# Two attention layers on one core: the output projections in halves, and an accumulating transfer in layer 1

## The chip, the cores and the metric

The kernel runs on one NeuronCore of a Trainium2 chip. The metric is the device time of one execution in microseconds (us), the median of several runs. The engines are TensorE (PE; its weight loads are PEld), VectorE (DVE), ScalarE (ACT), GpSimd (POOL) and SyncE (SP), each with its own instruction stream in program order; they meet by semaphores.

## The reference, cut to what matters

Two blocks follow each other on a sequence of 2048 tokens of width 128, with 16 heads of 64. Each is `x = x + attention(layernorm(x)) * silu(ffn(layernorm(x)))`. The attention of layer 0 is plain; that of layer 1 has rotated queries and keys and a distance bias per head. What this case is about is the last step of attention:

```python
attn = softmax(scores)                              # layer 1: softmax(scores + bias)
out  = einsum('bhqk,bhkd->bhqd', attn, v)
out  = out.transpose(0, 2, 1, 3).reshape(b, s, h * d) @ w_out   # sum over heads of o_h @ W_h
```

The product with the output weights is taken head by head, divided by the row sum of the softmax, and added up over the heads.

## The kernel before, in words

`attention_stage` runs once for each layer. A layer is a loop over 64 chunks (`NCH`), each one head and 512 queries (`NC` is 4 chunks per head, `LAST` is 63), and a chunk is 8 steps (`NS`) of 256 keys. Names: `st` are the scores in PSUM (two buffers), `jb` the PSUM scratch for the maxima, `ov` the attention output in PSUM, `osb` its copy in SBUF, `xb` one PSUM tile of 512 columns, `prob` a ring of six buffers of exponentials (printed as `room`), `acc` the accumulator of all tokens, `part` one chunk's scaled projection, `rs` the inverted row sums.

Each engine's order is written out by hand:

- TensorE, for every two steps: `maxima` two chunks ahead (L649, L650, into `jb`), `scores` (L683), `maxima`, then what `between` adds, then `values` of two steps earlier (L694). `between` has the three users of `xb`: `row(n+1)` in step 3 (L658) turns the chunk's maxima into a row, `sums_of(n-1)` in step 5 (L705) sums the exponentials over partitions, and `project(n-1)` in step 7 (L714) makes the four products of 128 by 128 with the output weights.
- VectorE: per step one maximum (L839 in layer 0, L834 with the bias in layer 1) and, in layer 1, the bias add from `st` into `prob` (L871); in layer 0 every second step a subtraction (L858). `merge` (L845) joins a chunk's maxima. `invert` (L877) makes `rs` from `xb`. In layer 0 `accumulate` (L886) reads `xb` in step 7 and adds it, scaled, to `acc`.
- ScalarE: `exponent` per step (L773, L777, L784), `divide_maxima` (L761) and `copy_out` (L791) in step 0, `row` (L766) in step 2, and in layer 1 `scale` (L798) in step 7, which writes `part` from `xb`.
- GpSimd: per chunk seven adds of 1024 columns over the exponentials (L991 six times, L994), one of 512 (L999), and in layer 1 `add_part` (L978), which adds `part` to `acc`.
- SyncE loads the next head's queries, keys and bias.

`xb` is shared, so its users wait for each other: `row` waits until the projection two chunks back has been read (`proj_done`), `sums_of` until the last one has been read, `copy_out` until the projection has read `osb` (`proj_ready`). `scale` waits until `part` has been added (`accumulated`). In the last chunk there are no maxima to make ahead, VectorE does part of GpSimd's adds (`close`, L912) and then the end: `gate_block` (L897) and `add_block` (L903).

Of the kernel before, what the change touches and what calls it, by code (L numbers as in the profile page):

```python
# [18 lines left out]
NC = S // QC  # L19
# [523 lines left out]
def attention_stage(nc, k, layer, heads, gate, bias=False, out=None):  # L543

    with ExitStack() as ctx:
# [38 lines left out]
        loads = low_loads + (1 if bias else 0)  # L584
        FIRST = AHEAD * NJ
        pool_adds = NS - 1
        block = ctx.enter_context(nc.Block())

        def scratch(n, j):
# [47 lines left out]
        def _(pe):  # L637
# [15 lines left out]
            def row(n):  # L653
                pe.wait_ge(m4_done, n + 1)
                if n >= 3:
                    pe.wait_ge(proj_done, n - 2)
                for t in range(4):
                    last = nc.tensor.matmul(xb[:, t * P:(t + 1) * P], m4w[:, t, :], k.ident16[:, :],  # L658
                                            start=True, stop=True)
                last.then_inc(row_ready, 1)  # L660
# [38 lines left out]
            def sums_of(n):  # L699
                pe.wait_ge(folded, n + 1)  # L700
                pe.wait_ge(row_done, min(n + 3, NCH))
                if n >= 1:
                    pe.wait_ge(proj_done, n)
                for q in range(4):
                    last = nc.tensor.matmul(xb[:, q:q + 1], total[:, q * P:(q + 1) * P], k.ones[:, 0:1],  # L705
                                            start=(q == 0), stop=True, skip_group_check=True)
                last.then_inc(sum_ready, 1)

            def project(n):
                pe.wait_ge(ov_saved, n + 1)  # L710
                pe.wait_ge(rs_done, n + 1)
                pe.wait_ge(row_done, min(n + 3, NCH))
                for q in range(4):
                    last = nc.tensor.matmul(xb[:, q * P:(q + 1) * P], osb[:, q * P:(q + 1) * P], k.wo[:, n // NC, :],  # L714
                                            start=True, stop=True)
                last.then_inc(proj_ready, 1)
# [12 lines left out]
            def between(n, s):  # L729
                if s == ROW_STEP and n + 1 < NCH:  # L730
                    row(n + 1)
                if s == SUM_STEP and n >= 1:
                    sums_of(n - 1)
                if s == OUT_STEP and n >= 1:
                    project(n - 1)

            for n in range(NCH):
                for s in range(NS):
# [9 lines left out]
                        values(*divmod(step - LAG + 1, NS))  # L748
            for s in range(NS - LAG, NS):
                values(NCH - 1, s)  # L750
            sums_of(NCH - 1)
            project(NCH - 1)

        @block.scalar
        def _(act):
            def divide_maxima(n):
                act.wait_ge(merged, n + 1)
                if n >= 1:
                    act.wait_ge(row_ready, n)
                wide = m4w[:, :, 0:DH + 1:DH] if bias else m4w[:, :, :]  # L760
                nc.scalar.activation(wide, m4[:, :].unsqueeze(2).broadcast_to([P, 4, 2 if bias else P]), ACT.Copy,  # L761
                                     scale=1.0 / MAXROW).then_inc(m4_done, 1)

            def row(n):
                act.wait_ge(row_ready, n + 1)
                nc.scalar.activation(rows[:, n % 2, :], xb[:, :], ACT.Copy).then_inc(row_done, 1)  # L766

            def exponent(n, s):
                step = NS * n + s
                r = step % RING  # L770
                if bias:
                    act.wait_ge(added, step + 1)
                    nc.scalar.activation(prob[:, r, :], prob[:, r, :], ACT.Exp, scale=k.sscale[:, layer:layer + 1])\  # L773
                       .then_inc(exp_done, 1)
                elif not by_row(step):
                    act.wait_ge(lowered, step // 2 + 1)
                    nc.scalar.activation(prob[:, r, :], prob[:, r, :], ACT.Exp, scale=k.sscale[:, 0:1])\  # L777
                       .then_inc(exp_done, 1)
                else:
                    act.wait_ge(st_ready, step + 1)  # L780
                    if step >= RING:
                        act.wait_ge(pv_done, step - RING + 1)
                        act.wait_ge(summed, summed_by(step - RING))
                    nc.scalar.activation(prob[:, r, :], st[:, step % 2, :], ACT.Exp, scale=k.sscale[:, layer:layer + 1])\  # L784
                       .then_inc(exp_done, 1)

            def copy_out(n):
                act.wait_ge(pv_done, NS * (n + 1))
                if n >= 1:
                    act.wait_ge(proj_ready, n)  # L790
                nc.scalar.activation(osb[:, :], ov[:, :], ACT.Copy).then_inc(ov_saved, 1)  # L791

            def scale(n):
                act.wait_ge(proj_ready, n + 1)
                if n >= 1:
                    act.wait_ge(accumulated, n)
                for q in range(4):
                    last = nc.scalar.activation(part[:, q * P:(q + 1) * P], xb[:, q * P:(q + 1) * P], ACT.Copy,  # L798
                                                scale=rs[:, q:q + 1])
                last.then_inc(proj_done, 1)  # L800

            act.wait_ge(ones_set, 2)
            nc.scalar.activation(osb[:, 0:1], k.ones[:, 0:1], ACT.Exp)
            divide_maxima(0)
            row(0)
            if bias:
                act.wait_ge(gathered, 16 * NT)
                for q in range(NT):
                    nc.scalar.activation(k.gate[:, q, :], k.gate[:, q, :], ACT.Silu, scale=k.prob[:, q:q + 1])
            for n in range(NCH):  # L810
                for s in range(NS):
                    if s == 0 and n + 1 < NCH:
                        divide_maxima(n + 1)
                    exponent(n, s)
                    if s == 0 and n >= 1:
                        copy_out(n - 1)
                    if s == ROW_STEP - 1 and n + 1 < NCH:
                        row(n + 1)
                    if bias and s == OUT_STEP and n >= 1:
                        scale(n - 1)  # L820
            copy_out(NCH - 1)

        @block.vector
        def _(ve):
# [48 lines left out]
            def invert(n):  # L873
                ve.wait_ge(sum_ready, n + 1)
                if n >= 1:
                    ve.wait_ge(proj_done, n)
                nc.vector.reciprocal(rs[:, :], xb[:, 0:4]).then_inc(rs_done, 1)  # L877

            def accumulate(n):
                ve.wait_ge(ones_set, 3)  # L880
                ve.wait_ge(proj_ready, n + 1)
                if bias:
                    ve.wait_ge(accumulated, n - NC + 1)
                for q in range(4):
                    a = k.acc[:, (n % NC) * 4 + q, :]
                    last = nc.vector.scalar_tensor_tensor(a, xb[:, q * P:(q + 1) * P], rs[:, q:q + 1], a,  # L886
                                                          ALU.mult, ALU.add)
                last.then_inc(proj_done, 1)

            def gate_block(i):  # L890
                block_end = LAST - NC + blocks[i].stop // 4
                if bias and block_end < LAST:
                    ve.wait_ge(accumulated, block_end + 1)
                else:
                    ve.wait_ge(proj_done, block_end + 1)
                tiles = blocks[i]
                nc.vector.tensor_tensor(k.acc[:, tiles, :], k.acc[:, tiles, :], gate[:, tiles, :], ALU.mult)\  # L897
                  .then_inc(finished, 1)
# [29 lines left out]
            for n in range(NCH):  # L928
                if n + 1 < NCH:
                    merge(n + 1)  # L930
                for s in range(NS):
# [6 lines left out]
                    if s == SUM_STEP and n >= 1:  # L938
                        invert(n - 1)
                    if not bias and s == OUT_STEP and n >= 1:  # L940
                        accumulate(n - 1)
                    if n == LAST and s in (6, 7):
                        close(s - 1)
            close(7)
# [4 lines left out]
            if bias:  # L949
                gate_block(1)  # L950
                add_block(1)
            accumulate(LAST)
            gate_block(len(blocks) - 1)
            add_block(len(blocks) - 1)

# [1 line left out]
        def _(pool):  # L957
# [13 lines left out]
            def add_part(n):  # L971
                if n == 0:
                    pool.wait_ge(ones_set, 3)
                pool.wait_ge(proj_done, n + 1)
                if n >= NC:
                    pool.wait_ge(accumulated, n - NC + 1)
                a = flat(k.acc[:, (n % NC) * 4:(n % NC + 1) * 4, :])
                nc.gpsimd.tensor_tensor(a, a, part[:, :], ALU.add).then_inc(accumulated, 1)  # L978

            for n in range(NCH):  # L980
                adds = (1, 3) if n == LAST else (1, 3, 4, 5, 6, 7)
                for i, s in enumerate(adds):
# [6 lines left out]
                        pool.wait_ge(folded, n)  # L989
                    first = a if i >= 2 else prob[:, (step - 1) % RING, :]  # L990
                    nc.gpsimd.tensor_tensor(a, first, prob[:, step % RING, :], ALU.add).then_inc(summed, 1)  # L991
                pool.wait_ge(summed, pool_adds * n + len(adds))
                a = sums[:, n % 2, :]
                nc.gpsimd.tensor_tensor(a, a, sums[:, (n + 1) % 2, :], ALU.add).then_inc(summed, 1)  # L994
                if n < LAST:
# [1 line left out]
                    if n >= 1:  # L997
                        pool.wait_ge(sum_ready, n)
                    nc.gpsimd.tensor_tensor(total[:, :], a[:, 0:QC], a[:, QC:2 * QC], ALU.add).then_inc(folded, 1)  # L999
                if bias and n >= 1:  # L1000
                    add_part(n - 1)


# [563 lines left out]
```

## Time and profile before

| | us |
|---|---|
| median of 3 runs (2865.01 to 2867.71) | 2866.11 |
| the profiled execution | 2865.61 |
| its span, first to last instruction | 2863.8 |
| PE busy / DVE / ACT / POOL | 2715.1 / 2453.7 / 1578.9 / 2459.9 |
| mean granted TensorE clock | 0.974 of full |

Layer 0's chunks lie between about 195 and 1360 us of the span, the feed-forward and rotation stages of layer 1 up to about 1580, and layer 1's chunks from about 1610 to 2850. Busy times are sums over stages with different limits, so the stages have to be looked at one by one. An idle time in square brackets is that of the engine just before the instruction, with what ended it; TensorE's matmuls overlap each other, so that its waits show on PEld or as gaps between starts.

### The profile page before, as it was taken

Reading aid. Unit: us, or ns where it says so; the run is one execution under the profiler, and the core shown is the slowest. Engines: PE = TensorE matmul, PEld = TensorE weight load, DVE = VectorE, ACT = ScalarE, POOL = GpSimd, SP = SyncE. Lnnn points to the kernel's source line nnn. Section 1 sums busy time; section 2 is a strip of 40 time slices with the busy share of each in tenths; the row PEclk is TensorE's granted clock in tenths of the full one; section 3 lists DMA queues with packets and bytes.
Section 4 is the critical chain, followed back from the end, with each engine's and each line's share of the span. In section 5 each row is a group of like instructions: output and inputs, shape, how many; then the busy total and the mean of one; then the engine's idle time right before and its main releaser. Section 6 shows DMA issues by size and latency. Waiting matters only on the chain. (4 is left out here: it accounts for less than half of the span.)

```text
span 2863.8 us, 46490 instructions
## 1 busy us (share of the span) xinstructions
PE 2715.1 (95%) x17528; PEld 1130.0 (39%) x17528; DVE 2453.7 (86%) x3263; ACT 1578.9 (55%) x1970; POOL 2459.9 (86%) x1179
## 2 busy tenths in 40 slices
PE   4899999999999999999589599999999999999998
PEld 3434334433343434433365133333333333333343
DVE  6578888888888888886678699999999999999997
ACT  4345555555555555555255355655565565555555
POOL 0219999999999999999245599999999999999998
PEclk8999999999999999999699699999999999999999
DMA  5441111111111111110323421111222222222200
GB/s 117 145 153 31 30 30 30 31 30 27 26 27 25 27 27 26 29 30 1 97 106 140 142 59 59 56 33 36 53 59 59 59 59 59 59 59 59 59 1 15
DMA packets 68864, 155.27 MB, mean 54 GB/s; under 512 B 20497, under 2 KB 34202, under 8 KB 66466
## 3 DMA queue, kind: packets, MB, share of 16 engines
q1 hardware_dynamic: 67618, 150.21, 18.8%
q8 instruction: 140, 2.29, 0.4%
q0 software_dynamic: 1024, 2.10, 0.2%
q14 instruction: 82, 0.67, 0.1%
HBM read 113.34 MB, written 38.93 MB: 53 GB/s over the span
## 5 line engine op out<-in xcount | busy, mean ns | idle before, releaser
L991 POOL TENSOR_TENSOR a_sums<-a_sums,room 128x1024 f32<-128x1024 f32 x504 | 1179.3, 2368 | 9.0 <-ACT room L773 3.7
L694 PE MATMUL a_ov<-room,va 128*64 128x512 f32 x4096 | 991.6, 605 | 0.6 <-ACT room L773 0.6
L773 ACT ACTIVATE room<-room,sscale 128x1024 f32<-128x1024 f32 x512 | 588.4, 1149 | 493.5 <-DVE room L871 493.3
L839 DVE TENSOR_REDUCE a_mx<-a_jb 128x1 f32<-128x1024 f32 x496 | 606.0, 1222 | 180.3 <-PE a_jb L650 180.1
L991 POOL TENSOR_TENSOR a_sums<-room 128x1024 f32<-128x1024 f32 x256 | 604.2, 2362 | 62.1 <-ACT room L777 35.2
L834 DVE CUSTOM_DVE_ANT_0 a_junk<-a_jb,a_tab 128x1024 bf16<-128x1024 f32 x501 | 609.3, 1216 | 49.0 <-DVE a_m L845 36.3
L871 DVE TENSOR_TENSOR room<-a_st,a_tab 128x1024 f32<-128x1024 f32 x512 | 623.8, 1220 | 14.2 <-PE a_st L683 14.2
L777 ACT ACTIVATE room<-room,sscale 128x1024 f32<-128x1024 f32 x256 | 294.0, 1148 | 351.7 <-DVE room L858 351.7
L649 PE MATMUL a_jb<-a_kh,a_qh 64*128 64x512 f16 x997 | 384.5, 386 | 14.2 <-DVE a_mx L834 3.1
L694 PEld LDWEIGHTS a_ov<-room,va 128*64 128x64 f32 x4096 | 248.4, 136 | 363.2 <-issue 295.2
L683 PE MATMUL a_st<-a_qh,a_kh 64*128 64x512 f16 x2048 | 390.1, 378 | 0.1
L683 PE MATMUL a_st<-a_ql,a_kh 64*128 64x512 f16 x2048 | 389.2, 377 | 0.0
L683 PE MATMUL a_st<-a_qh,a_kl 64*128 64x512 f16 x2048 | 389.2, 377 | 0.0
L650 PE MATMUL a_jb<-a_kh,a_qh 64*128 64x512 f16 x997 | 384.5, 386 | 0.0
L858 DVE SCALAR_TENSOR_TENSOR room<-a_rows,a_st 128x1024 f32<-128x1024 f16 x256 | 309.8, 1210 | 15.9 <-PE a_st L683 15.9
L649 PEld LDWEIGHTS a_jb<-a_kh,a_qh 64*128 64x128 f16 x997 | 92.5, 93 | 579.3 <-issue 197.3
L994 POOL TENSOR_TENSOR a_sums<-a_sums 128x1024 f32<-128x1024 f32 x128 | 304.6, 2380 | 10.0
L784 ACT ACTIVATE room<-a_st,sscale 128x1024 f32<-128x1024 f32 x256 | 282.6, 1104 | 38.8 <-POOL a_sums L991 29.1
L683 PE MATMUL a_st<-a_rows,a_lower 64*128 64x512 f16 x1536 | 292.1, 377 | 0.0
L999 POOL TENSOR_TENSOR a_total<-a_sums 128x512 f32<-128x512 f32 x126 | 160.4, 1273 | 9.9
L714 PE MATMUL a_xb<-wo,a_osb 128*128 128x128 f32 x1024 | 150.0, 290 | 1.1 <-issue 1.1
L683 PEld LDWEIGHTS a_st<-a_qh,a_kl 64*128 64x128 f16 x2048 | 99.8, 94 | 121.9 <-issue 1.0
(241 smaller groups left out, 2546.3 us busy)
## 6 DMA issues: line engine op xcount, KB each, us to landing
a_tab<-bias_line SPq DMA_DIRECT2D x16, 1984.0 KB, 9.1
qk_high<-room SPq DMA_DIRECT2D x16, 512.0 KB, 2.6
qk_low<-room SPq DMA_DIRECT2D x16, 512.0 KB, 3.6
a_qh<-qk_high SPq DMA_DIRECT2D x32, 256.0 KB, 4.5
a_kh<-qk_high SPq DMA_DIRECT2D x32, 256.0 KB, 5.1
a_ql<-qk_low SPq DMA_DIRECT2D x32, 256.0 KB, 6.8
a_kl<-qk_low SPq DMA_DIRECT2D x32, 256.0 KB, 7.1
qk_high<-er_split SPq DMA_DIRECT2D x32, 256.0 KB, 2.1
```

The source lines that it names most:

```text
L649: nc.tensor.matmul(o[:, 0:QC], qh[0:DH, q0:q0 + P], kh[0:DH, k0:k0 + QC], start=True, stop=True)
L650: nc.tensor.matmul(o[:, QC:2 * QC], qh[DH:P, q0:q0 + P], kh[DH:P, k0 + QC:k0 + 2 * QC], start=True, stop=True).then_inc(max_ready, 1)
L683: last = nc.tensor.matmul(st[:, step % 2, t * QC:(t + 1) * QC], w, x, start=(r == 0), stop=(r == len(rounds) - 1))
L694: last = nc.tensor.matmul(ov[t * DH:(t + 1) * DH, :], k.va[:, 2 * s + t, h * DH:(h + 1) * DH], prob[:, step % RING, t * QC:(t + 1) * QC], ...
L773: nc.scalar.activation(prob[:, r, :], prob[:, r, :], ACT.Exp, scale=k.sscale[:, layer:layer + 1])\
L777: nc.scalar.activation(prob[:, r, :], prob[:, r, :], ACT.Exp, scale=k.sscale[:, 0:1])\
L834: nc.vector.tensor_tensor_reduce(out=junk[:, i % 2, :], in0=scratch(n, j), in1=tab[:, n // NC % 2, c0:c0 + 2 * QC][:, ::-1], scale=1.0, sc ...
L839: nc.vector.reduce_max(mx[:, n % 2, j // 2, j % 2:j % 2 + 1], scratch(n, j), AX.X).then_inc(max_done, 1)
L858: nc.vector.scalar_tensor_tensor(p, high, -float(MAXROW), x, ALU.mult, ALU.add).then_inc(lowered, 1)
L871: nc.vector.tensor_tensor(p[:, :, ::-1], x[:, :, ::-1], window, ALU.add).then_inc(added, 1)
L991: nc.gpsimd.tensor_tensor(a, first, prob[:, step % RING, :], ALU.add).then_inc(summed, 1)
L994: nc.gpsimd.tensor_tensor(a, a, sums[:, (n + 1) % 2, :], ALU.add).then_inc(summed, 1)
```

## The change: what it does, and the diff

A chunk's projection is made in two halves of two products. The first half stays in step 7 of the following chunk; the second is made in step 1 of the chunk after that. The reader of `xb` (VectorE's `accumulate` in layer 0, ScalarE's `scale` in layer 1) is halved in the same way. `proj_ready` and `proj_done` now count halves. In the last chunk both halves are made in step 7, and at the end both follow each other. In layer 1, `part` is no longer added to `acc` by a GpSimd instruction, but by a transfer that GpSimd issues and that adds on arrival; it stands behind GpSimd's first add of the chunk two later, and `accumulated` counts in steps of 16.

```diff
+        HALVES = ((0, 1), (2, 3))
+        parts = len(HALVES)
...
             def row(n):
                 pe.wait_ge(m4_done, n + 1)
                 if n >= 3:
-                    pe.wait_ge(proj_done, n - 2)
+                    pe.wait_ge(proj_done, parts * (n - 2))
...
-            def project(n):
+            def project(n, half):
                 pe.wait_ge(ov_saved, n + 1)
                 pe.wait_ge(rs_done, n + 1)
-                pe.wait_ge(row_done, min(n + 3, NCH))
-                for q in range(4):
+                pe.wait_ge(row_done, min(n + 3, NCH) if half == 0 else min(n + 2, NCH))
+                if half == 1:
+                    pe.wait_ge(proj_done, parts * n + 1)
+                for q in HALVES[half]:
...
                 if s == OUT_STEP and n >= 1:
-                    project(n - 1)
+                    project(n - 1, 0)
+                if n == LAST and s == OUT_STEP:
+                    project(n - 1, 1)
+                if n >= 2 and s == 1:
+                    project(n - 2, 1)
...
-            project(NCH - 1)
+            sums_of(LAST)
+            for half in range(parts):
+                project(LAST, half)
...
-            def scale(n):
-                act.wait_ge(proj_ready, n + 1)
+            def scale(n, half):
+                act.wait_ge(proj_ready, parts * n + half + 1)
                 if n >= 1:
-                    act.wait_ge(accumulated, n)
-                for q in range(4):
+                    act.wait_ge(accumulated, 16 * n)
+                for q in HALVES[half]:
...
                     if bias and s == OUT_STEP and n >= 1:
-                        scale(n - 1)
+                        scale(n - 1, 0)
+                        if n == LAST:
+                            scale(n - 1, 1)
+                    if bias and s == 1 and n >= 2:
+                        scale(n - 2, 1)
...
                     if not bias and s == OUT_STEP and n >= 1:
-                        accumulate(n - 1)
+                        accumulate(n - 1, 0)
+                        if n == LAST:
+                            accumulate(n - 1, 1)
+                    if not bias and s == 1 and n >= 2:
+                        accumulate(n - 2, 1)
...
-                nc.gpsimd.tensor_tensor(a, a, part[:, :], ALU.add).then_inc(accumulated, 1)
+                nc.gpsimd.dma_start(a, part[:, :], accum_op=ALU.add).then_inc(accumulated, 16)
...
                     nc.gpsimd.tensor_tensor(a, first, prob[:, step % RING, :], ALU.add).then_inc(summed, 1)
+                    if bias and i == 0 and n >= 2:
+                        add_part(n - 2)
...
-                if bias and n >= 1:
+                if bias and n == LAST:
                     add_part(n - 1)
```

The other lines of the diff put `parts *` or `16 *` before the counts that are waited for.

## Rows read from the trace of the kernel before

**Rows 1.** Page, part 1: busy time, share of span, instructions.
```profile
PE 2715.1 (95%) x17528; PEld 1130.0 (39%) x17528; DVE 2453.7 (86%) x3263; ACT 1578.9 (55%) x1970; POOL 2459.9 (86%) x1179
```

**Rows 2.** Windows, layer 0 and layer 1: us, busy (x) by engine, PEclk, DMA.
```profile
...
700.00:1100.00 400.00, 399.75 (x2728) 159.81 (x2726) 336.37 (x397) 228.93 (x242) 386.18 (x176) 1.00 0.15 33
2000.00:2400.00 400.00, 397.86 (x2736) 156.51 (x2734) 384.07 (x539) 237.46 (x313) 391.90 (x188) 1.00 0.21 61
```

**Rows 3.** Groups, layer 1, 1600 to 2700: the repeating work.
```profile
...
L834 DVE CUSTOM_DVE_ANT_0 a_junk<-a_jb,a_tab 128x1024 bf16<-128x1024 f32 x453 | 551.0, 1216 | 45.0 <-DVE a_m L845 33.3 <-PE a_jb L650 11.7
L871 DVE TENSOR_TENSOR room<-a_st,a_tab 128x1024 f32<-128x1024 f32 x449 | 547.6, 1220 | 0.4 <-PE a_st L683 0.4
L991 POOL TENSOR_TENSOR a_sums<-a_sums,room 128x1024 f32<-128x1024 f32 x224 | 526.1, 2370 | 8.1 <-ACT room L773 3.4
...
L994 POOL TENSOR_TENSOR a_sums<-a_sums 128x1024 f32<-128x1024 f32 x55 | 130.3, 2369 | 4.3
...
L999 POOL TENSOR_TENSOR a_total<-a_sums 128x512 f32<-128x512 f32 x55 | 70.0, 1272 | 4.3
```

**Rows 4.** Timeline, layer 1, one period: start, us, instruction, [idle, releaser].
```profile
...
2200.47 1.15 ACT L773 ACTIVATE room<-room,sscale 128x1024 f32<-128x1024 f32 x1 [0.36 <-DVE room L871]
...
2201.63 0.09 PEld L649 LDWEIGHTS a_jb<-a_kh,a_qh 64*128 64x128 f16 x1 [0.59 <-DVE a_mx L834]
...
2201.95 0.40 PE L658 MATMUL a_xb<-ident,a_m4w 128*128 128x128 f16 x4
...
2202.57 1.29 POOL L978 TENSOR_TENSOR acc<-acc,a_part 128x512 f32<-128x512 f32 x1
...
2209.78 1.22 DVE L834 CUSTOM_DVE_ANT_0 a_junk<-a_jb,a_tab 128x1024 bf16<-128x1024 f32 x1 [0.16 <-PE a_jb L650]
...
2211.62 1.16 PE L714 MATMUL a_xb<-wo,a_osb 128*128 128x128 f32 x8
...
2215.10 1.22 DVE L834 CUSTOM_DVE_ANT_0 a_junk<-a_jb,a_tab 128x1024 bf16<-128x1024 f32 x1 [0.61 <-DVE a_m L845]
...
2215.52 1.12 ACT L798 ACTIVATE a_part<-a_xb,a_rs 128x128 f32<-128x128 f32 x4
...
2216.39 0.09 PEld L649 LDWEIGHTS a_jb<-a_kh,a_qh 64*128 64x128 f16 x1 [0.19 <-DVE a_mx L834]
...
2216.84 1.94 PE L694 MATMUL a_ov<-room,va 128*64 128x512 f32 x8
...
2218.82 0.60 ACT L791 ACTIVATE a_osb<-a_ov 128x512 f32<-128x512 f32 x1 [0.17 <-PE a_ov L694]
...
2221.26 0.40 PE L658 MATMUL a_xb<-ident,a_m4w 128*128 128x128 f16 x4
```

**Rows 5.** Timeline, layer 0, around the accumulate.
```profile
...
802.60 0.09 PEld L649 LDWEIGHTS a_jb<-a_kh,a_qh 64*128 64x128 f16 x1 [0.38 <-DVE a_mx L839]
...
814.45 1.12 DVE L886 SCALAR_TENSOR_TENSOR acc<-a_xb,a_rs,acc 128x128 f32<-128x128 f32 x4
...
815.56 1.22 DVE L839 TENSOR_REDUCE a_mx<-a_jb 128x1 f32<-128x1024 f32 x1
...
816.83 0.09 PEld L649 LDWEIGHTS a_jb<-a_kh,a_qh 64*128 64x128 f16 x1 [0.39 <-DVE a_mx L839]
```

**Rows 6.** Timeline, GpSimd, one gather behind another, and the landing of all 16.
```profile
...
1586.63 0.95 POOL L968 DMA_INDIRECT gate<-sorted_out,spot  x1 [0.30 <-issue]
...
DMA to landing us min/median/max: 2.6/4.2/8.2
```

**Rows 7.** Timeline, layer 1, the end, and its granted clock (windows).
```profile
...
2844.35 1.16 PE L714 MATMUL a_xb<-wo,a_osb 128*128 128x128 f32 x8
...
2848.73 1.12 ACT L798 ACTIVATE a_part<-a_xb,a_rs 128x128 f32<-128x128 f32 x4
...
2848.00:2852.00 4.00, 1.31 (x6) 0.20 (x4) 3.86 (x3) 2.45 (x6) 2.81 (x2) 0.95 0.00 0
```

More of the change, by code:

```diff
@@ L702, in sums_of @@
                 if n >= 1:
-                    pe.wait_ge(proj_done, n)
+                    pe.wait_ge(proj_done, parts * n)
                 for q in range(4):
@@ L750, in _ @@
                 values(NCH - 1, s)
-            sums_of(NCH - 1)
-            project(NCH - 1)
+            sums_of(LAST)
+            for half in range(parts):
+                project(LAST, half)
         @block.scalar
@@ L789, in copy_out @@
                 if n >= 1:
-                    act.wait_ge(proj_ready, n)
+                    act.wait_ge(proj_ready, parts * n)
                 nc.scalar.activation(osb[:, :], ov[:, :], ACT.Copy).then_inc(ov_saved, 1)
-            def scale(n):
-                act.wait_ge(proj_ready, n + 1)
+            def scale(n, half):
+                act.wait_ge(proj_ready, parts * n + half + 1)
                 if n >= 1:
-                    act.wait_ge(accumulated, n)
-                for q in range(4):
+                    act.wait_ge(accumulated, 16 * n)
+                for q in HALVES[half]:
                     last = nc.scalar.activation(part[:, q * P:(q + 1) * P], xb[:, q * P:(q + 1) * P], ACT.Copy,
@@ L875, in invert, with accumulate @@
                 if n >= 1:
-                    ve.wait_ge(proj_done, n)
+                    ve.wait_ge(proj_done, parts * n)
                 nc.vector.reciprocal(rs[:, :], xb[:, 0:4]).then_inc(rs_done, 1)
-            def accumulate(n):
+            def accumulate(n, half):
                 ve.wait_ge(ones_set, 3)
-                ve.wait_ge(proj_ready, n + 1)
+                ve.wait_ge(proj_ready, parts * n + half + 1)
                 if bias:
-                    ve.wait_ge(accumulated, n - NC + 1)
-                for q in range(4):
+                    ve.wait_ge(accumulated, 16 * (n - NC + 1))
+                for q in HALVES[half]:
                     a = k.acc[:, (n % NC) * 4 + q, :]
@@ L892, in gate_block @@
                 if bias and block_end < LAST:
-                    ve.wait_ge(accumulated, block_end + 1)
+                    ve.wait_ge(accumulated, 16 * (block_end + 1))
                 else:
-                    ve.wait_ge(proj_done, block_end + 1)
+                    ve.wait_ge(proj_done, parts * (block_end + 1))
                 tiles = blocks[i]
@@ L951, in _ @@
                 add_block(1)
-            accumulate(LAST)
+            for half in range(parts):
+                accumulate(LAST, half)
             gate_block(len(blocks) - 1)
@@ L973, in add_part @@
                     pool.wait_ge(ones_set, 3)
-                pool.wait_ge(proj_done, n + 1)
+                pool.wait_ge(proj_done, parts * (n + 1))
                 if n >= NC:
-                    pool.wait_ge(accumulated, n - NC + 1)
+                    pool.wait_ge(accumulated, 16 * (n - NC + 1))
                 a = flat(k.acc[:, (n % NC) * 4:(n % NC + 1) * 4, :])
-                nc.gpsimd.tensor_tensor(a, a, part[:, :], ALU.add).then_inc(accumulated, 1)
+                nc.gpsimd.dma_start(a, part[:, :], accum_op=ALU.add).then_inc(accumulated, 16)
             for n in range(NCH):
```

## The prediction

> **What bounds the kernel now.** I read the views in this order: the page's first part, the windows by stage, the groups of layer 1, then one period of each layer in the timeline, and last the end of layer 1.
>
> TensorE is the busiest engine by name [rows 1], but the windows show two different regimes [rows 2]. In layer 0 TensorE is busy for 399.75 of 400 us and VectorE for 336. In layer 1 four engines' worth of pressure meet: TensorE 398, VectorE 384 and GpSimd 392 of 400. A share does not say who waits for whom there, so the period has to be walked.
>
> One chunk of layer 1 takes 2221.26 - 2201.95 = 19.31 us, from one row transpose (L658) to the next [rows 4]. VectorE does eight pairs of maximum (1216 ns, less the overlap of neighbours) and bias add (1220 ns) [rows 3], nearly back to back. It stands idle twice: 0.61 us behind its own merge and 0.16 us before the maximum at 2209.78, which waits for TensorE's a_jb [rows 4]. So the period is a ring through several engines. From 2209.78 VectorE works without a break worth naming until the bias add of the next step 1. From there TensorE takes over: a_jb at 2201.63, the row transpose at 2201.95, then values, scores and sums in fixed order until the a_jb that releases 2209.78. From the row transpose to that maximum it is 7.83 us, and every delay of the transpose arrives at VectorE in full, since VectorE is already 0.16 us ahead of it.
>
> GpSimd in layer 1 does six adds (2370 ns), one of 2369, one of 1272 and the part's add of 1.29 us [rows 3, 4]: 14.22 + 2.37 + 1.27 + 1.29 = 19.15 of 19.31 us. It is full, but I count it as following: its first add of a chunk comes after the part's add at 2202.57, though the exponential that it reads was ready at 2200.47 + 1.15 = 2201.62; and no idle of VectorE in [rows 4] is put down to it.
>
> **The change part by part.**
>
> *Part's add leaves GpSimd (layer 1).* 1.29 us of a queue on which nothing waits go away: worth nothing while the ring above sets the period. In its place stands the issue of an accumulating transfer. No row shows one. The nearest is the indirect gather: 0.95 us and 0.30 us until the next, so 1.25 us [rows 6]. Below, it can't cost less than nothing; above, I allow twice the gather, 2.5 us, since it reads a source and a target. I take 1.25. GpSimd then holds 17.86 + 1.25 = 19.1 us.
>
> *Landing.* The issue comes behind GpSimd's first add, so near 2202.57 + 2.37 = 2204.9; landing after 2.6 to 8.2 us [rows 6] gives 2213.1 at the latest. The next scale, which now waits for it, stands at 2215.52 [rows 4]: hidden by 2.4 us at the worst landing. If that cover goes, ScalarE stalls with the exponential of step 0, the divided maxima and copy-out queued behind it.
>
> The Trainium skill ("SBUF — State Buffer", section "SBUF: two separate sides") warns that descriptors of a transfer issued by GpSimd can't be written while VectorE runs a 2-port instruction. By its condition this would not bite: the two big VectorE instructions of layer 1 each take one operand from PSUM (a_jb, a_st) and one from SBUF. By the rule biting, the issue would be longer by about one VectorE instruction; that is rival 2 below, with its own price from rows.
>
> *Project in step 7 shrinks.* Eight records take 1.16 us [rows 4], a half about 0.58. TensorE is early by 0.54 to 0.58 at the next a_jb, but VectorE's maximum at 2215.10 waits for the merge (0.61 us idle), not for TensorE [rows 4]. Gain in layer 1: zero.
>
> *Project in step 1 is added.* It stands between the a_jb of step 1 (2216.39) and values (2216.84). TensorE arrives there 0.15 us or more earlier than now, held by VectorE's maximum instead; values move by about 0.45 us, and copy-out from 2218.82 to about 2219.25. It then ends at 2219.85, while the exponential of step 1 is due at 2200.47 + 19.31 = 2219.78, with instructions on ScalarE starting up to 0.1 us before the last one's end: just covered. The a_jb behind values follows near 2219.2; VectorE's maximum of step 2, two pairs (some 2.3 us each) behind the one at 2215.10, wants it complete by 2219.7. It is, with nothing to spare.
>
> *The new wait: the row transpose behind scale.* This is what I expect to decide. row(n+1) in step 3 waits for the projections through n-2 to be read out of xb. Until now that was done in step 7 of the chunk before. Now the last half is scaled in step 1, by ScalarE, in order behind the exponential of step 1. That one ends at 2200.47 + 1.15 = 2201.62. Four scales take 1.12 us, each some 0.36 at the end of a pitch of 0.253 us, so two take 0.61 us: done at 2202.23, with a pass to TensorE near 2202.25. The transpose stood at 2201.95 [rows 4]. It is late by 0.3, or by 0.2 if ScalarE starts the scale 0.1 us before the exponential's end. Queued behind it on TensorE are values, scores, sums and the a_jb for which VectorE already waits. I take 0.27 us; bounds 0.1 and 0.6 (copy-out late too). It applies to chunks 2 to 61, 60 of them, where maxima are still made: 60 x 0.27 = +16 us.
>
> *Layer 0.* Here VectorE reads xb. Its four accumulates take 1.12 us at 814.45 in front of the maximum at 815.56, which ends at 816.78; TensorE's a_jb follows at 816.83 [rows 5], 0.05 behind. Half the accumulates gone (0.51 us) brings this forward by as much as the half project brings TensorE forward (0.55). In step 1 TensorE gets the 0.55 back and VectorE the 0.51, in front of the maximum after which a_jb stands at 802.60 [rows 5]. The two halves cancel. The row transpose is not hit: VectorE has read xb before that same maximum, over 1 us earlier. What is left is the start of a second fp32 block on TensorE, 0 to 0.1 us; I take 0.05 x 60 = +3 us. A gain of up to 0.1 us per chunk is not excluded, if both small waits vanish.
>
> *Chunk 63.* Both halves of a projection now follow each other with a read-out between. In layer 0 VectorE waits twice for a half project (0.58 us, more at the lower clock) with hand-overs: about +1.5 us. In layer 1 the half at 2844.35 ends at 2844.93; the second waits for a scale behind the last exponentials, 2848.73 + 0.61 = 2849.34 [rows 7]. TensorE is idle for 4.4 us; the last 16 records of values, 3.7 us at the pace of [rows 4] (8 in 1.94, less the tail), end at 2853.6, just before the sums at 2854.14. But the granted clock fell from 1.00 to 0.95 within 2848 to 2852 [rows 7], when TensorE paused for lack of work, and those sums took 1.87 us. At the lower of the two levels (1.2 GHz) the values take 7.4 us and end after 2857, 3.2 us late. With +1.2 for the final pair of halves the end costs 1.2 to 4.5; I take 3.
>
> **Sum:** 16 + 3 + 1.5 + 3 = +23.5 us on the profiled execution's 2865.6 (span 2863.8 and 1.8 around it), which lies 0.5 below the median of 2866.1: **2889 us**, +0.8%. Own range: 2876 to 2903.
>
> **Rivals.**
>
> 1. *The row wait is hidden.* If ScalarE reads out the half before TensorE gets to the row, or VectorE's lead is larger than 0.16 us, the 16 falls to under 3. Speaks for it: the margin is a quarter of a microsecond. Against: the exponential's end and the transpose are 0.33 us apart and two scales take 0.61. Time 2865.6 + 3 + 1.5 + 3 = 2873, down to 2869.
>
> 2. *GpSimd becomes the bound.* It has 17.86 us of adds left; with a period of 19.58 and 0.15 us of own waits it decides from an issue of 1.55 us. At 1.9 us the period is 19.9: +0.6 x 62 = 37, plus 7.5, 2910. At 2.5 us it would be 20.5: +1.2 x 62 = 74, 2947. Against it: the gather's 1.25. For it: a second read per element. If the skill's port rule bit, this is where it would show.
>
> 3. *Faster.* One mechanism: the accumulates in front of VectorE's maximum hold TensorE in layer 0 (the a_jb at 816.83 follows that maximum's end by 0.05). If halving them frees TensorE and the half in step 1 fits without pushing the next maximum, 0.11 us x 60 = 6.6 us come back; with the row wait hidden as in rival 1 and both ends at their least (2.5), the time is 2861.5, and under 2860 from 0.14 us per chunk. It decides only if the row wait costs under 0.03 us.
>
> 4. *The transfer lands late*, beyond 2215.5, at the 15 head changes when the loads share the DMA engines: +2 us each, 2920 together with the main case.
>
> **Chances.** Forecast 0.62; rival 1 0.15; rival 2 0.12; rival 3 0.05; rival 4 0.03; something else 0.03. What a measurement of this kernel tells from no change is 0.2%, 5.7 us: 2860.4 to 2871.8. Faster 0.06 (rival 3 and a little of the rest); same 0.14, of rival 1 and the lower side of the forecast; slower 0.80. The range 2868 to 2906 holds rival 1 in most of its width and the forecast, and leaves out rivals 2 and 3.
>
> **What would show it.** Right: ScalarE's scale as two groups of half the count; in layer 1 the row transpose or its weight load waits for ScalarE L798's line by 0.2 to 0.3 us, 60 times; the idle of VectorE's maximum behind a_jb grows from 0.16 to about 0.45 us a chunk; period 19.6; layer 0 unchanged within 0.1; GpSimd in layer 1 below its 98% now, with waits. Wrong: no wait of the transpose on ScalarE; GpSimd still without idle and the period above 19.8 (rival 2); ScalarE waiting for a DMA (rival 4).

## The result, and the profile after

The changed kernel takes 2877.4 us in the median (2876.4 to 2877.7, five runs) against 2865.7 us: the ratio is 1.004 (95% interval 1.0029 to 1.0052), 11.7 us slower. A sixth execution, disturbed (granted clock 0.666), is left out. The forecast was slower by 23.5 us, to 2889, with a range of 2868 to 2906. The time lies in the range and moved in the direction that was forecast; the size is twice what was measured, and the stage in which the loss was to lie is the wrong one.

Of the page of the changed kernel, its part 1 (busy time and share by engine) and the row of the new transfer (count, size, microseconds to landing):

```profile
PE 2724.2 (95%) x17528; PEld 1147.4 (40%) x17528; DVE 2466.7 (86%) x3263; ACT 1560.1 (54%) x1970; POOL 2430.1 (85%) x1179
...
acc<-a_part POOLq DMA_DIRECT2D x63, 256.0 KB, 3.3
```

GpSimd has 30 us less to do than in [rows 1] and TensorE 9 us more, with the same number of matmuls. To see where the time went, one instruction is followed that every chunk has once, ScalarE's copy of the row (L766 before, L775 after). The view of this line gives count, durations, and its first and last start; first the kernel before, layer 0 and layer 1, then the changed one:

```profile
...
L766 ACT ACTIVATE a_rows<-a_xb x60: 583/586/588, 239.3 to 1313.4; 128x512 f16<-128x512 f32 x60
...
L766 ACT ACTIVATE a_rows<-a_xb x60: 573/576/579, 1663.1 to 2802.5; 128x512 f16<-128x512 f32 x60
```

```profile
...
L775 ACT ACTIVATE a_rows<-a_xb x59: 594/594/595, 240.2 to 1302.6; 128x512 f16<-128x512 f32 x59
...
L775 ACT ACTIVATE a_rows<-a_xb x61: 572/577/578, 1655.7 to 2810.6; 128x512 f16<-128x512 f32 x61
```

First to last start, divided by the count less one, is the period: layer 0 (1313.4 - 239.3) / 59 = 18.21 us before, (1302.6 - 240.2) / 58 = 18.32 after; layer 1 (2802.5 - 1663.1) / 59 = 19.31 before, (2810.6 - 1655.7) / 60 = 19.25 after. Layer 1, where I looked for 16 us of loss, has become a little faster. With the starts of the same instruction and of the second layer norm as marks, the two profiled spans (2863.8 and 2875.7) part into these stretches:

| stretch | before, us | after, us | difference |
|---|---|---|---|
| start to row copy 3 of layer 0 | 239.3 | 240.2 | +0.9 |
| 59 chunks of layer 0 | 1074.2 | 1080.7 | +6.6 |
| last chunks of layer 0, to the layer norm | 55.6 | 57.8 | +2.2 |
| between the layers, to row copy 0 of layer 1 | 236.6 | 239.4 | +2.8 |
| first three chunks of layer 1 | 57.5 | 56.7 | -0.8 |
| 59 chunks of layer 1 | 1139.4 | 1135.9 | -3.5 |
| last chunk of layer 1 and the end | 61.4 | 65.1 | +3.7 |

**Layer 1.** One period in the timeline of the changed kernel, the instructions that answer to [rows 4] (start, us, instruction, in brackets the idle before it and what ended it):

```profile
...
2205.12 0.09 PEld L651 LDWEIGHTS a_jb<-a_kh,a_qh 64*128 64x128 f16 x1 [0.81 <-issue]
...
2205.35 0.15 DVE L858 TENSOR_REDUCE a_m<-a_mx 128x4 f32<-128x8 f32 x1
...
2205.65 1.23 DVE L847 CUSTOM_DVE_ANT_0 a_junk<-a_jb,a_tab 128x1024 bf16<-128x1024 f32 x1 [0.16 <-DVE a_m L858]
...
2210.51 1.14 ACT L782 ACTIVATE room<-room,sscale 128x1024 f32<-128x1024 f32 x1
...
2211.55 0.61 ACT L807 ACTIVATE a_part<-a_xb,a_rs 128x128 f32<-128x128 f32 x2
...
2211.85 0.38 PE L651 MATMUL a_jb<-a_kh,a_qh 64*128 64x512 f16 x1
...
2212.30 0.38 PE L660 MATMUL a_xb<-ident,a_m4w 128*128 128x128 f16 x4
...
2215.17 0.86 POOL L996 DMA_DIRECT2D acc<-a_part  x1
...
2219.60 0.09 PEld L651 LDWEIGHTS a_jb<-a_kh,a_qh 64*128 64x128 f16 x1 [0.81 <-issue]
...
2220.03 1.23 DVE L847 CUSTOM_DVE_ANT_0 a_junk<-a_jb,a_tab 128x1024 bf16<-128x1024 f32 x1 [0.38 <-PE a_jb L652]
```

Two idle times of VectorE are to be compared. Before a chunk's first maximum (2205.65) there are now 0.16 us where there were 0.61. Before the maximum of step 6 (2220.03) there are 0.38 where there were 0.16. The views of waits in layer 1 (waiter, releaser: us in total, times, longest) say the same, first before, then after:

```profile
...
DVE a_junk L834 <- DVE a_m L845: 33.3, 55, 0.6
...
DVE a_junk L834 <- PE a_jb L650: 11.7, 58, 1.5
```

```profile
...
DVE a_junk L847 <- PE a_jb L652: 22.7, 57, 1.5
...
DVE a_junk L847 <- DVE a_m L858: 8.5, 54, 0.2
```

The name of the releaser misleads. The 0.61 us were put down to VectorE's own merge, but the merge does the same work after the change and costs 0.16. Two more rows of the kernel before, from the same chunk as [rows 4], give the reason:

```profile
...
2214.35 0.15 DVE L845 TENSOR_REDUCE a_m<-a_mx 128x4 f32<-128x8 f32 x1
...
2214.57 0.39 PE L649 MATMUL a_jb<-a_kh,a_qh 64*128 64x512 f16 x1
```

The merge ends at 2214.50. TensorE's a_jb starts at 2214.57 and takes 0.39, so the maximum that reads it can't start before 2214.96, and it started at 2215.10. The wait had two conditions, and by these rows TensorE's was the later one. The end of a matmul is modelled in the profile, so this is a reading to be tested; e6 below does it.

The row transpose (L660) starts at 2212.30, behind a scale that ends at 2211.55 + 0.61 = 2212.16 and behind an a_jb at 2211.85. Before, the transpose followed its a_jb by 0.32 [rows 4]; now it is 0.45. So the wait that I predicted exists, at 0.13 us instead of 0.27.

**Layer 0.** The rows that answer to [rows 5]:

```profile
...
818.96 0.60 DVE L899 SCALAR_TENSOR_TENSOR acc<-a_xb,a_rs,acc 128x128 f32<-128x128 f32 x2
...
819.08 0.09 PEld L651 LDWEIGHTS a_jb<-a_kh,a_qh 64*128 64x128 f16 x1 [0.81 <-issue]
...
819.59 1.23 DVE L852 TENSOR_REDUCE a_mx<-a_jb 128x1 f32<-128x1024 f32 x1
...
820.87 0.09 PEld L651 LDWEIGHTS a_jb<-a_kh,a_qh 64*128 64x128 f16 x1 [0.38 <-DVE a_mx L852]
...
821.19 0.71 PE L718 MATMUL a_xb<-wo,a_osb 128*128 128x128 f32 x4
...
821.83 0.20 PEld L696 LDWEIGHTS a_ov<-room,va 128*64 128x64 f32 x4
```

The accumulate takes 0.60 us instead of 1.12, and from the a_jb ahead of it to the next one there are 1.79 us (weight loads at 819.08 and 820.87), against 1.81 in the kernel before (815.02 and 816.83): the step of the accumulate has hardly become shorter. The block of project, four records, starts at 821.19, and values follow at 821.83: 0.64 us. In the kernel before, the block of eight started at 812.07 and values behind it at 813.16: 1.09. Two halves hold TensorE for 1.28, 0.19 more than the whole.

**The ends.** In layer 0's chunk 63, TensorE waits in step 7 for VectorE's first two accumulates. In the timeline of the changed kernel the second half-block starts with 1.78 us of idle before it:

```profile
...
1363.96 0.60 DVE L899 SCALAR_TENSOR_TENSOR acc<-a_xb,a_rs,acc 128x128 f32<-128x128 f32 x2
...
1364.70 0.68 PE L718 MATMUL a_xb<-wo,a_osb 128*128 128x128 f32 x4 [1.78 <-DVE acc L899]
...
1365.32 3.65 PE L696 MATMUL a_ov<-room,va 128*64 128x512 f32 x16
```

In layer 1's chunk 63 it waits for ScalarE. The timeline of the changed kernel:

```profile
...
2858.80 0.60 ACT L807 ACTIVATE a_part<-a_xb,a_rs 128x128 f32<-128x128 f32 x2
...
2859.55 1.10 PE L718 MATMUL a_xb<-wo,a_osb 128*128 128x128 f32 x4 [4.86 <-ACT a_part L807]
...
2860.58 4.87 PE L696 MATMUL a_ov<-room,va 128*64 128x512 f32 x16
```

The view of windows, 2860 to 2864 (us, busy and count by engine PE, PEld, DVE, ACT, POOL, then the granted clock, 0.62 of full, a mix of the two levels 1.2 and 2.4 GHz):

```profile
...
2860.00:2864.00 4.00, 4.00 (x16) 1.41 (x15) 3.23 (x4) 0.62 (x2) 0.87 (x1) 0.62 0.26 49
```

TensorE idles for 4.86 us, and the 16 records of values that follow take 4.87 us, where [rows 4] has eight in 1.94 at full clock.

**The transfer.** Its issue on GpSimd and its landing in the changed kernel:

```profile
...
L996 POOL DMA_DIRECT2D acc<-a_part x63: 842/861/989, 1676.1 to 2861.6; - x63
...
DMA to landing us min/median/max: 3.2/3.3/10.3
```

The issue costs 0.86 us and lands after 3.3 us in the median, 10.3 at worst. Of the 63 landings 49 take at most 4.5 us and 14 take 8.4 or more; these 14 are one head change apart, each with SyncE's loads for the next head still under way. The next scale of step 7 starts 10.6 us behind the issue (2215.17 to 2225.77), so that the worst landing is hidden by 0.3 us only (issue 2022.65, landing 10.3 us later, scale 2033.25). In the changed kernel nothing waits for it. In e2 below, which has the same layer 1, one landing took 11.7 us, and ScalarE waited for it:

```profile
...
2163.45 0.85 POOL L996 DMA_DIRECT2D acc<-a_part  x1
...
2175.23 0.63 ACT L807 ACTIVATE a_part<-a_xb,a_rs 128x128 f32<-128x128 f32 x2 [1.10 <-DMA acc<-a_part]
```

That one chunk took 1.07 us longer than its neighbours. In e8 and e9 one chunk each is longer in the same way, by 0.19 and 0.67 us.

### The profile page after: what moved, and what is told of

Read it like the earlier page. It is cut to its first block and busy times, and to the rows that moved or that the text cites. A ratio compares the mean times of both kernels' runs of the same rounds, so it can differ in the third digit from the quotient of the medians.

```text
span 2875.7 us, 46873 instructions
## 1 busy us (share of the span) xinstructions
PE 2724.2 (95%) x17528; PEld 1147.4 (40%) x17528; DVE 2466.7 (86%) x3263; ACT 1560.1 (54%) x1970; POOL 2430.1 (85%) x1179
## 5 line engine op out<-in xcount | busy, mean ns | idle before, releaser
L718 PE MATMUL a_xb<-wo,a_osb 128*128 128x128 f32 x1024 | 183.8, 303 | 10.9 <-DVE acc L899 5.2
L800 ACT ACTIVATE a_osb<-a_ov 128x512 f32<-128x512 f32 x128 | 76.4, 597 | 187.5 <-PE a_ov L696 187.5
L718 PEld LDWEIGHTS a_xb<-wo,a_osb 128*128 128x128 f32 x1024 | 135.0, 192 | 90.2 <-issue 90.2
```

## The experiments

All medians stand beside runs of the kernel before on the same chip. Theory A is what the trace of the changed kernel suggests, B is my prediction's reading, C gives the gain of layer 1 to the work taken off GpSimd. A's periods for e1 and e2 are taken from that trace, so these two runs test whether the layers can be looked at apart; from e3 on the numbers are forecasts. A period here is the median time from one row copy to the next, which a single late chunk does not move: by it the kernel before has 18.20 and 19.31 us and the changed one 18.32 and 19.25. (From first to last row copy e2 has 19.27 in layer 1, for its one late chunk.)

| kernel | median us | before there | ratio (95%) | layer 0 period | layer 1 period |
|---|---|---|---|---|---|
| e1, halves in layer 0 alone | 2875.3 | 2865.6 | 1.0033 (1.0021 to 1.0046) | 18.32 | 19.31 |
| e2, layer 1 alone | 2866.2 | 2865.6 | 1.0000 (0.9991 to 1.0009) | 18.20 | 19.25 |
| e3, layer 1 without the transfer | 2867.5 | 2865.6 | 1.0005 (0.9996 to 1.0014) | 18.20 | 19.25 |
| e4, transfer alone | 2864.6 | 2865.6 | 0.9995 (0.9986 to 1.0004) | 18.20 | 19.31 |
| e5, one more block in layer 0 | 2886.1 | 2866.0 | 1.0074 (1.0058 to 1.0089) | 18.56 | 19.31 |
| e6, half of layer 1's products left out | 2836.9 | 2866.0 | 0.9900 (0.9885 to 0.9915) | 18.20 | 18.86 |
| e7, earlier scale | 2859.1 | 2866.0 | 0.9978 (0.9969 to 0.9987) | 18.20 | 19.12 |
| e8, whole ends | 2853.3 | 2866.0 | 0.9958 (0.9945 to 0.9972) | 18.20 | 19.12 |
| e9, only the read-out halved in layer 0 | 2853.9 | 2866.4 | 0.9955 (0.9942 to 0.9969) | 18.18 | 19.12 |

### Which layer loses: e1 and e2

```diff
-        HALVES = ((0, 1), (2, 3))
+        HALVES = ((0, 1), (2, 3)) if not bias else ((0, 1, 2, 3),)     # e1; e2 has: if bias
```

With one part the calls for a second half fall away; e1 also has GpSimd's add at its old place.

> Halves in layer 0 alone; layer 1 as in the kernel before (one projection in step 7, GpSimd's add). Theory A (a second block of projection costs TensorE its start and end again, some 0.2 us per chunk, of which layer 0 gets back the two small gaps of 0.1): layer 0's period 18.32 us instead of 18.21, its last chunk 2 us longer, layer 1's period 19.31 as before, in all 2866 + 0.75 + 6.9 + 2.0 = 2875.4. Theory B (my prediction: layer 0 nearly free, the loss sits in layer 1 behind ScalarE): layer 0's period 18.21 to 18.26, in all 2867 to 2871.

> Layer 0 as in the kernel before; layer 1 in halves and with the accumulating transfer. Theory A: layer 1's period 19.25 us (0.06 less than before), its end 3 us longer, in all 2866 - 3.6 + 3.0 = 2865.4, the same as before. Theory B: period 19.5 or more and 2880 or more.

Both came out as A has it: 2875.3 and 2866.2, with periods of 18.32 and 19.31, and 18.20 and 19.25. (The terms of A's sum for e1 add up to 2875.65 and not to 2875.4.) Layer 0 alone carries 9.7 of the 11.7 us, and layer 1's change is worth nothing in sum, since its end gives back what its chunks win. Together the two runs have 10.3 of the 11.7 us; the rest is within their intervals. B falls for both layers.

### What the transfer does: e3 and e4

```diff
-                nc.gpsimd.dma_start(a, part[:, :], accum_op=ALU.add).then_inc(accumulated, 16)
+                nc.gpsimd.tensor_tensor(a, a, part[:, :], ALU.add).then_inc(accumulated, 1)   # e3, on e2
```

e4 is the kernel before with the opposite edit, at the old place in GpSimd's order.

> As the run with layer 1 alone in halves, but the part is added by GpSimd's own instruction at the new place instead of the transfer. Theory A (layer 1's 0.06 us come from TensorE, which is early at step 0): period 19.25 us, the same total as with the transfer, within 2 us. Theory C (they come from the 1.3 us taken off GpSimd): period back to 19.31 us or above, since GpSimd then has 19.15 us of work in 19.25, and 3.5 us or more longer than with the transfer.

> The kernel before, but with the accumulating transfer in place of GpSimd's add, at the old place in its order; nothing in halves. Theory A: layer 1's period 19.31 us, GpSimd with some 0.4 us of idle per chunk, in all 2866 within 2 (the end 1 us shorter at best). Theory C: period 19.25 or less, 2862 or less.

The period does not ask for the transfer: 19.25 with and without it once the projection is in halves, 19.31 with and without it otherwise. C falls. In total, e2 and e3 differ by 1.3 us and e4 lies 1.0 under the kernel before, each with intervals that overlap; the profile shows where something of that size would come from, in the last chunk. First e4, then the kernel before:

```profile
...
2850.16 0.87 POOL L996 DMA_DIRECT2D acc<-a_part  x1 [1.40 <-ACT a_part L807]
2851.21 1.23 DVE L930 TENSOR_TENSOR a_qh<-a_qh,a_sums 128x1024 f32<-128x1024 f32 x1
```

```profile
...
2849.93 2.34 POOL L978 TENSOR_TENSOR acc<-acc,a_part 128x512 f32<-128x512 f32 x1 [1.19 <-ACT a_part L798]
...
2851.19 2.17 DVE L917 TENSOR_TENSOR a_qh<-a_qh,a_sums 128x1024 f32<-128x1024 f32 x1
```

GpSimd's add of the part lasts until 2852.27 and so runs beside the first 1.08 us of VectorE's addition of two tensors in SBUF, which takes 2.17 us. In e4 the transfer's issue is over at 2851.03, the transfer itself is under way until 2853.42, and the same addition takes 1.23.

### Is it the block, or the records: e5

```diff
+            def again(n):
+                pe.wait_ge(proj_done, n + 1)
+                pe.wait_ge(row_done, n + 3)
+                nc.tensor.matmul(xb[:, 0:P], osb[:, 0:P], k.wo[:, n // NC, :], start=True, stop=True)
...
+                if not bias and n >= 2 and s == 1:
+                    again(n - 2)
```

> The kernel before, with one more product of the finished projection (two records, its result in xb is not read) in layer 0's step 1, as a block of its own. The trace of the changed kernel gives 1.09 us from the start of a block of eight records to what follows and 0.65 from one of four, so 0.11 per record and 0.2 per block. Theory A (a block has a fixed cost of 0.2 us): 0.42 us of TensorE, less the 0.05 us gap before the a_jb of step 3, so layer 0's period 18.20 + 0.37 = 18.57, and 62 x 0.37 = 23 us in all: 2889. Theory B (cost proportional to the records, 0.136 each): 0.22 per chunk, 18.42, 2879.

The period came out at 18.56, where A had 18.57 and B 18.42; the total rose by 20.1 us, where 60 chunks of 0.36 would be 21 and A had said 23. The new block of two records in e5's timeline, with its neighbours:

```profile
...
827.76 0.39 PE L651 MATMUL a_jb<-a_kh,a_qh 64*128 64x512 f16 x1
...
828.08 0.49 PE L725 MATMUL a_xb<-wo,a_osb 128*128 128x128 f32 x2
...
828.50 1.94 PE L696 MATMUL a_ov<-room,va 128*64 128x512 f32 x8
```

Two records hold TensorE from 828.08 to 828.50, 0.42 us; four take 0.64 and eight 1.09. That is 0.11 per record and 0.2 per block.

### What ended VectorE's idle time: e6

```diff
-                for q in HALVES[half]:
+                for q in HALVES[half][:2 if bias else 4]:
```

In layer 1 the other two products are left out, and the scale reads all four quarters.

> Layer 1's projection makes only two of its four products (the scale still reads all four quarters); one block in step 7, with the accumulating transfer at the old place, layer 0 as before. Theory A (VectorE's 0.61 us of idle before the first maximum of a chunk ends with TensorE's a_jb, not with the merge that the view names): that idle falls to 0.16 and layer 1's period from 19.31 to 18.87 us, 2865 - 27 = 2838. Theory B (my prediction: the merge ends that idle, so TensorE's time in step 7 is worth nothing): period 19.31, 2865.

A had 18.87 and 2838; measured are 18.86 and 2836.9. The transfer that e6 carries too is not the cause: with it alone the period stays at 19.31 (e4). The waits of VectorE in layer 1 in this kernel:

```profile
...
DVE a_junk L847 <- PE a_jb L652: 10.6, 58, 0.9
...
DVE a_junk L847 <- DVE a_m L858: 8.8, 56, 0.2
```

Before the first maximum 8.8 us in 56 chunks are left, 0.16 each, as after the change. Making TensorE 0.44 us shorter in step 7 shortens the chunk by 0.45: this is the step of my prediction that failed.

### How much the row transpose waits: e7

```diff
+                    if bias and parts == 2 and s == 0 and n >= 2:
+                        scale(n - 2, 1)
                     if s == 0 and n >= 1:
                         copy_out(n - 1)
...
-                    if bias and parts == 2 and s == 1 and n >= 2:
-                        scale(n - 2, 1)
```

> Layer 1 alone in halves with the transfer, and ScalarE's second half of scale moved from behind the exponential of step 1 to before copy-out in step 0, where ScalarE is idle for 0.8 us. Theory A (the row transpose does wait for that scale, but only 0.1 us of it count, since TensorE itself is later by then): layer 1's period 19.15 instead of 19.25, 2866 - 6 = 2860. Theory D (the wait is hidden; TensorE's own order sets the transpose): 19.25, 2866. By the size that I predicted for the wait (0.27): 19.0, 2850.

The period is 19.12 (A: 19.15, D: 19.25, the predicted size: 19.0), the median 2859.1 against A's 2860. The timeline of e7:

```profile
...
2194.74 0.61 ACT L807 ACTIVATE a_part<-a_xb,a_rs 128x128 f32<-128x128 f32 x2
...
2195.64 0.60 ACT L800 ACTIVATE a_osb<-a_ov 128x512 f32<-128x512 f32 x1 [0.29 <-PE a_ov L696]
...
2197.49 0.38 PE L651 MATMUL a_jb<-a_kh,a_qh 64*128 64x512 f16 x1
...
2197.80 0.40 PE L660 MATMUL a_xb<-ident,a_m4w 128*128 128x128 f16 x4
...
2205.54 1.23 DVE L847 CUSTOM_DVE_ANT_0 a_junk<-a_jb,a_tab 128x1024 bf16<-128x1024 f32 x1 [0.29 <-PE a_jb L652]
```

The scale now ends at 2195.35, just ahead of copy-out, and the transpose follows its a_jb by 0.31 again. The period is 0.13 shorter than e2's 19.25, as much as the transpose had been late behind its a_jb (0.45 against 0.32). Of it 0.09 are in VectorE's wait in step 6, which has gone from 0.38 to 0.29; the rest is at the maximum of step 4, the first whose a_jb comes behind the transpose. The wait is not back at 0.16; I put what remains down to TensorE's own second block, which no run separates.

### The ends whole: e8

```diff
-                if half == 1:
+                if half == 1 and n < LAST - 1:
                     pe.wait_ge(proj_done, parts * n + 1)
...
-                act.wait_ge(proj_ready, parts * n + half + 1)
+                act.wait_ge(proj_ready, parts * n + half + 1 if n < LAST - 1 else parts * (n + 1))
```

VectorE's accumulate waits in the same way.

> As the run with the earlier scale, but the last two projections of layer 1 are made without the read-out between their halves, as one block each. The end of layer 1 (last row transpose to the end) falls from 46.5 to 43.5 us or less: 3 us less than the run with the earlier scale, 2857 by theory A.

Last row copy to the end: 42.8 us, with 46.8 in e7 and 43.5 in the kernel before. The end is 4.1 us shorter, where I expected 3. The median fell by 5.8 us to 2853.3; the profiled execution, at 2858.7 the longest of the five, also has the longest stretch between the layers (below), so that the whole spans of the two profiles differ by 0.8 us alone. The 4.1 are read from the end itself. The timeline of e8:

```profile
...
2838.42 1.16 PE L718 MATMUL a_xb<-wo,a_osb 128*128 128x128 f32 x8
...
2843.82 1.12 ACT L807 ACTIVATE a_part<-a_xb,a_rs 128x128 f32<-128x128 f32 x4
...
2843.97 1.08 PE L696 MATMUL a_ov<-room,va 128*64 128x512 f32 x4 [1.67 <-ACT room L782]
```

Eight records in one block again, and values wait 1.67 us for exponentials instead of 4.86 for a scale.

### Only the read-out in halves: e9

```diff
-                if half == 1 and n < LAST - 1:
+                if bias and half == 1 and n < LAST - 1:
...
+                    if not bias and s == 0 and n >= 2:
+                        accumulate(n - 2, 1)
```

In layer 0 both halves of project are made behind each other in step 7, and `accumulate` waits for both.

> Layer 1 as in the run with whole ends. Layer 0: the projection is one block again in step 7, and only VectorE's read-out is halved, two accumulates in step 7 and two in the next chunk's step 0, where VectorE is idle for 0.49 us before its second maximum. Theory A (layer 0 pays for the second block alone, 0.2 us, and gets back the gap of 0.06 us that the accumulates leave before the a_jb of step 1): layer 0's period 18.14 us instead of 18.20, 62 x 0.06 = 4 us less than with whole ends, 2849.5. Theory E (halving the accumulates gives nothing back, and layer 0's loss of 0.12 per chunk was smaller than 0.2 for another reason): 18.20, 2853.3.

18.18 lies nearer to E's 18.20 than to A's 18.14, and the total is that of e8. The timeline of e9 says why:

```profile
...
815.23 0.39 PE L651 MATMUL a_jb<-a_kh,a_qh 64*128 64x512 f16 x1
...
815.73 1.23 DVE L852 TENSOR_REDUCE a_mx<-a_jb 128x1 f32<-128x1024 f32 x1 [0.41 <-PE a_jb L652]
...
817.01 0.39 PE L651 MATMUL a_jb<-a_kh,a_qh 64*128 64x512 f16 x1
```

VectorE is now early, idle for 0.41 us until the a_jb. Still the next a_jb comes 1.78 us after the first, and it came 1.80 after it in the kernel before: copy into `jb`, maximum (1.23 us) and the next copy follow each other over one buffer. The accumulates had cost 0.02 there and not 0.06.

## Why the prediction was right or wrong

**The step that failed.** "Project in step 7 shrinks ... Gain in layer 1: zero", since the maximum "waits for the merge (0.61 us idle), not for TensorE". It waited for TensorE. Of the 0.61 us, 0.45 were TensorE's (e6: 18.86 instead of 19.31), which makes a gain of 0.45 us per chunk that my sum lacks, 27 us over 60 chunks. Row for row it could have been seen: a_jb at 2214.57 and 0.39 us of duration against a merge that was over at 2214.50. The profile puts a wait for several semaphores down to one of them, and I read the name without checking the time of the other candidate.

**The row wait.** The mechanism was right and mis-sized: a scale behind the exponential in step 1, and the transpose behind it. Predicted 0.27, measured 0.13 of period (e2 against e7). That every delay of the transpose arrives at VectorE in full holds: 0.13 later behind its a_jb, 0.13 of period. I timed the transpose where it had been, but the half block in step 1 makes TensorE itself later by then (the a_jb before it at 2211.85 starts behind scores and no longer right at the release by VectorE), so half of the scale's lateness was covered.

**Layer 1 together.** -0.45 from step 7; +0.22 more wait in step 6, in which most of the row wait's 0.13 lies; +0.12 where the maximum of step 2 starts late (2210.33 against 2210.21, when the bias add before it lets go), which I had called complete in time "with nothing to spare". The rest of some 0.05 lies mostly at the maximum of step 4, the first whose a_jb comes behind the transpose. In all -0.06 us per chunk, -3.5 us, where the sum had +16.

**Layer 0.** The start of a second fp32 block was allowed 0 to 0.1 us, taken as 0.05; it is 0.2. Of it the changed kernel gets back 0.06 before the a_jb of step 3 and 0.02 before that of step 1, so 0.12 per chunk remain: 6.6 us for 59 chunks instead of 3. I bounded a block's start by the transitions between blocks and forgot its end: in the block of four the records hold TensorE for 0.21, 0.11, 0.11 and 0.20 us, the first and the last twice as long as those between. For the same reason a half holds it for 0.64 us and not for the 0.58 that I took as half of 1.16.

**Chunk 63.** Predicted 1.5 and 3. Measured 2.2 and 3.7, each with the last period before it. The clock did fall, as forecast, but for the first part of the values alone (0.62 in 2860 to 2864), so that they took 4.87 and not 7.4 us.

**The transfer.** The issue takes 0.86 us, where I took 1.25, and GpSimd is no bound in either form (e3): rival 2 is refuted. The landing took up to 10.3 us, where I had 8.2 as the worst, and was hidden by 0.3 us instead of 2.4. Rival 4 is wrong in size, 2 us at each of 15 head changes, but its mechanism exists: long landings at the head changes, and in e2 one of them cost 1.07 us. The rule of the Trainium skill that rival 2 was set beside ("SBUF — State Buffer", section "SBUF: two separate sides") was not put to the test: its condition, a 2-port instruction of VectorE, was by the prediction's own reading not met. No issue took longer than 0.99 us. Rival 1 named the right stage for the wrong reason: the row wait isn't hidden, it is outweighed.

**The right direction for partly wrong reasons.** Slower came true through layer 0 and the ends (+6.6, +2.2, +3.7), three terms that the sum held at 7.5 together; the term of 16 that decided the forecast stands against -3.5 for the whole of layer 1's chunks. The measured time lies in the range because losses elsewhere were put too low, and not because of the row wait: as far as layer 1 goes, that is luck.

**Left open.** The 236.6 to 239.4 us between the layers, which the change does not touch. In the eleven profiles this stretch lies between 235.0 and 240.5, the extremes in e5 and e8, whose edits don't touch it either, so I take the 2.8 us for scatter. The same goes for the start (238.6 to 240.4 us to row copy 3) and layer 1's first three chunks (56.6 to 57.7), with +0.9 and -0.8. That these are independent of the change is argued and not shown; without them the table explains 9.0 of the 11.9 us between the two profiles.

## What to carry to other kernels

A wait's releaser in a profile is a name and not a proof: put the end of each condition (here the merge's 2214.50 and the a_jb's 2214.57 + 0.39) beside the start of the waiter before a stall is priced. When a block of small fp32 matmuls is split, count a start and an end for each part, and ask at which point of the ring TensorE is late: here taking 0.45 us of TensorE's time away from one such point was worth 0.45 in layer 1, while in layer 0, where TensorE waits for some 0.12 us per chunk, the split got back 0.08 of the 0.2 that it costs. Halves that are read out in turn need their cover in the last iteration too; here they were better made whole there (e8). With layer 0 left whole, the earlier scale and whole ends, e8 is 12.7 us under the kernel before, where the change as made was 11.7 above it. And a transfer's cover has to be measured against its longest landing and not the median one: 3.3 us in the median, and 11.7 once in e2, which was 1.10 us too long.

## What the runs showed of the hardware

- A block of fp32 matmuls of 128 by 128 between other work holds TensorE for 0.42 us with two records (e5), 0.64 with four (the changed kernel) and 1.09 with eight (the kernel before).
- An accumulating transfer of 256 KB within SBUF takes GpSimd 0.86 us to issue (0.84 to 0.99) and lands after 3.3 us in the median. With the loads of the next head under way it took 8.4 us and more, up to 10.3 in the changed kernel and 11.7 in e2.
- VectorE's addition of two SBUF tensors of 128x1024 took 2.17 us when a GpSimd addition ran beside its first 1.08 us, and 1.23 while a transfer was under way whose issue was over.
- After 4.86 us without work, TensorE's granted clock was 0.62 in the window from 2860 to 2864 us, and 16 records of values took 4.87 us instead of 3.65 (the same 16 in layer 0's last chunk, after 1.78 us of idle).
